# Bands of the first layer's attention: a quarter read back in one whole transfer instead of four partial ones

## The reference

```
logits  = bond_logits - 10.0 * damage            # [b, head, t, 64], of gelu(strain @ W ...)
logits  = where(t - 63 + j >= 0, logits, -inf)
weights = softmax(logits, axis=-1)               # over the window, j = 0..63
out     = einsum('bntd,bntde->bnte', weights, val_win)   # val_win[t, j] = val[t - 63 + j]
x = x + out @ W_cproj + ffn(xn)                  # ffn: 16 experts, top 4
```

## Time and profile before

| what | us |
|---|---|
| median of 3 runs (1136.08 to 1141.26) | 1139.98 |
| the profiled execution, its own time | 1139.31 |
| its span | 1137.6 |
| PE busy in the span | 974.3 |
| DVE busy | 909.8 |
| ACT busy | 787.7 |
| POOL busy | 561.9 |
| band stage of group 0 | 301.4 to 376.6 |
| band stage of group 1 | 626.0 to 707.3 |

### The profile page before, as it was taken

One profiled execution on the slowest core, in us unless ns is written; L12 is line 12 of the kernel. 1 busy time (PEld: TensorE's weight loads), 2 busy tenths in 40 slices (PEclk: granted clock), 3 DMA queues, 4 the chain that ended last, 5 costly groups with the idle time before them and its releaser, 6 DMA issues. The chain is left out here.

```text
span 1137.6 us, 23649 instructions
## 1 busy us (share of the span) xinstructions
PE 974.3 (86%) x9302; PEld 519.0 (46%) x9302; DVE 909.8 (80%) x1006; ACT 787.7 (69%) x859; POOL 561.9 (49%) x571
## 2 busy tenths in 40 slices
PE   5787778889778799999987688998999999989897
PEld 3522222233467344333333578634645465555533
DVE  7888888899777999999996867677686667476857
ACT  3689999999764899999997532432366656555574
POOL 6088888528637558888886523407720000000172
PEclk9889999999989999999999688997799999999999
DMA  8891011012188212222210784000314344432121
GB/s 292 229 376 37 31 36 33 22 39 67 39 226 193 77 58 72 71 73 73 74 55 34 203 218 118 4 1 22 98 49 130 94 120 139 122 102 84 38 59 45
DMA packets 102597, 109.56 MB, mean 96 GB/s; under 512 B 11893, under 2 KB 87121, under 8 KB 98769
## 3 DMA queue, kind: packets, MB, share of 16 engines
q1 hardware_dynamic: 93492, 87.67, 26.8%
q0 software_dynamic: 7424, 20.20, 5.9%
q10 hardware_dynamic: 1571, 0.20, 0.1%
HBM read 62.29 MB, written 42.59 MB: 92 GB/s over the span
## 5 line engine op out<-in xcount | busy, mean ns | idle before, releaser
L262 DVE SCALAR_TENSOR_TENSOR ring<-AD,PT 128x1808 f32<-128x1808 f32 (+15 forms) x128 | 282.2, 2221 | 28.1 <-PE LG L985 27.3
L985 PE MATMUL LG<-ring,lred 128*32 128x456 f32 (+15 forms) x2048 | 237.2, 583 | 0.0
L268 POOL DMA_INDIRECT ys<-rows,goali x80 | 162.1, 2027 | 72.3 <-DVE rows L869 49.4
L2362 DVE TENSOR_REDUCE MX<-SS 128x2 f32<-128x1024 f32 x119 | 144.5, 1218 | 55.6 <-PE SS L2079 55.5
L2292 ACT ACTIVATE EX<-SS 128x1024 f32<-128x1024 f32 x128 | 130.3, 1031 | 79.3 <-PE SS L2079 78.8
L925 ACT ACTIVATE ring<-ring 128x3680 f32<-128x3680 f32 (+15 forms) x47 | 161.2, 3429 | 3.6 <-DVE ring L262 3.6
L1010 PE MATMUL SD<-DSf,eyes 99*32 99x456 bf16 (+15 forms) x1280 | 96.3, 377 | 66.4 <-ACT ring L930 63.1
L931 ACT ACTIVATE ring<-ring 128x1824 f32<-128x1824 f32 (+15 forms) x80 | 145.8, 1822 | 0.0
L1996 POOL DMA_INDIRECT XN<-ys,sloti x16 | 16.4, 1024 | 246.8 <-PE SS L2089 242.2
L778 POOL DMA_INDIRECT xs<-rows,sloti x64 | 121.7, 1902 | 30.5 <-issue 19.2
L985 PEld LDWEIGHTS LG<-ring,lred 128*32 128x32 f32 x2048 | 61.5, 111 | 99.1 <-issue 76.2
(11 more groups left out here) (434 smaller groups left out, 1720.6 us busy)
## 6 DMA issues: line engine op xcount, KB each, us to landing
w1s<-in_L_ffn_W SPq DMA_DIRECT2D x39, 256.0 KB, 3.0
w2s<-in_L_ffn_W SPq DMA_DIRECT2D x39, 256.0 KB, 3.0
band<-Z SPq DMA_DIRECT2D x8, 1024.0 KB
xl<-xs SPq DMA_DIRECT2D x20, 272.0 KB, 3.1
xs<-Z SPq DMA_DIRECT2D x5, 1024.0 KB, 9.7
w1s<-w1d SPq DMA_DIRECT2D x80, 64.0 KB
w2s<-w2d SPq DMA_DIRECT2D x80, 64.0 KB
ring<-band SPq DMA_DIRECT2D x12, 384.0 KB, 9.5
```

The lines of the kernel that those rows point to most:

```text
L262: return v.scalar_tensor_tensor(out=tile[:, s, :, t0:T], in0=AD[:, s, :, j + t0:j + T], scalar=extra, in1=AD[:, s, :, PAD + t0:PAD + T], o ...
L268: pool.indirect_dma_start(ys0[:, :], bass.IndirectOffsetOnAxis(ap=goali[:, 4 * n + a:4 * n + a + 1], axis=0), yo[:, n % 2, a, :], None, bo ...
L985: mm = pe.matmul(LG[32 * b:32 * b + 32, par, s, t0:T], lred[:, s, n % 4, :], ring[:, slot, s, b, t0:T], start=(n % 4 == 0), stop=(n % 4 == 3))
L2362: v.tensor_reduce(MX[:, t, p // 2, hh:hh + 2], pairs_of(b, name), AX.X, ALU.max).then_inc(freed[slot], 1)
```

## The change

`read(k)` becomes one DMA, issued by SP: all 128 rows of `band[k]`, 128 slots each, 2 MB, over 128 partitions of 16 KB. POOL issues no band reads any more. Since every slot of `wide` is now written, the clearing of the three buffers and its semaphore go. The semaphores `d_band_in` are one per quarter instead of two. POOL's other work closes up: in group 0 both stores come first, in group 1 all eight `gate_rows` stand in a row.

```diff
-            def landed(k, half):
-                return d_in[k][half], 16 * (64 // BLK) * (g + 1)
+            def landed(k):
+                return d_in[k], 16 * (g + 1)
...
-            def read(engine, k, half):
+            def read(sp, k):
-                engine.wait_ge(wide_zero, WIDE * g + min(k, WIDE - 1) + 1)
                 if k >= WIDE:
-                    engine.wait_ge(band_pe, 8 * (M0 + k - WIDE + 1))
-                engine.wait_ge(*written(k))
-                for s0 in range(0, 64, BLK):
-                    r0 = 64 * half + s0
-                    rows = dram_rows(band, (k * P + r0) * 32 * P + 32 * s0, [[32 * P, BLK], [1, 32 * SPAN]])
-                    engine.dma_start(wide[k % WIDE][r0:r0 + BLK, s0:s0 + SPAN, :].rearrange("r s n -> r (s n)"), rows
-                                     ).then_inc(landed(k, half)[0], 16)
+                    sp.wait_ge(band_pe, 8 * (M0 + k - WIDE + 1))
+                sp.wait_ge(*written(k))
+                sp.dma_start(wide[k % WIDE].rearrange("r s n -> r (s n)"), band[k]).then_inc(landed(k)[0], 16)
...
-                clear(0)
                 if g == 0:
                     store(pool, MOE[0][7][0])
-                clear(1)
-                if g == G - 1:
-                    gate_rows(pool, 0, 0)
-                    gate_rows(pool, 0, 1)
-                read(pool, 0, 1)
-                clear(2)
-                read(pool, 1, 1)
-                if g == 0:
                     store(pool, MOE[0][7][1])
                 else:
-                    gate_rows(pool, 1, 0)
-                    gate_rows(pool, 1, 1)
-                for k in range(2, NT):
-                    read(pool, k, 1)
-                if g == G - 1:
-                    for k in range(2, K0):
+                    for k in range(K0):
                         for half in range(2):
                             gate_rows(pool, k, half)
...
-                read(sp, 0, 0)
+                read(sp, 0)
                 write(1)
-                read(sp, 1, 0)
-                for half in range(2):
-                    sp.wait_ge(*landed(0, half))
+                read(sp, 1)
+                sp.wait_ge(*landed(0))
                 write(2)
                 write(3)
                 for k in range(2, NT):
-                    read(sp, k, 0)
+                    read(sp, k)
```

More of the change, by code:

```diff
@@ L49 @@
 WIDE = 3
-BLK = 32
-SPAN = BLK + WIN
 PE_ITEMS = (1, 2, 4, 5, 7)
@@ L637, in first_layer @@
     d_out = [sem(f"d_skew{k}") for k in range(NT)]
-    d_in = [[sem(f"d_band_in{k}_{half}") for half in range(2)] for k in range(NT)]
+    d_in = [sem(f"d_band_in{k}") for k in range(NT)]
     band_pe, band_act, band_dve, vw_pe, vw_sb, nd_pe, rc_ready, att_ready = (
         sem(n) for n in ("band_pe", "band_act", "band_dve", "vw_pe", "vw_sb", "nd_pe", "rc_ready", "att_ready"))
-    wide_zero, vp_zero, side_pe, side_sb = sem("wide_zero"), sem("vp_zero"), sem("side_pe"), sem("side_sb")
+    vp_zero, side_pe, side_sb = sem("vp_zero"), sem("side_pe"), sem("side_sb")
     rct_sb = sem("rct_sb")
@@ L1429, in turn @@
                         if i == 0:
-                            for half in range(2):
-                                pe.wait_ge(*landed(k, half))
+                            pe.wait_ge(*landed(k))
                         before = max(4 * m + i // 2 - 1, 0)
```

2 lines of the change are left out of this document (removed).

## The result

The changed kernel takes **1129.88 us** (median of 5 runs, 1128.16 to 1132.02), the kernel before 1139.98 (5 runs, 1136.08 to 1141.26): a ratio of 0.991, 95% interval 0.989 to 0.993, 10.1 us less. Forecast were 1131.3 and 8.7 us. The profiled execution of the changed kernel took 1132.02 us, its span 1130.3 (1139.3 and 1137.6 before).

The account below looks back on a forecast made before the run. Read(2)'s landing, behind one queue of band transfers, was taken to bound each stage. With r (moving a 2.10 MB read) at 5.5 us, gains 19.5 - 3r and 22.2 - 3r sum to 8.7 us: 1131.3 us, range 1126.5 to 1139.5.

Parts of the forecast that it names:

- The rate: Both band stages: a whole 2.10 MB read over 128 partitions moves in 5.5 us, at 381 GB/s.
- Fixed time ahead of a read: Issue and landing cost about 1.9 us beyond movement, paid before read(0) and read(1), where the queue is empty.
- w: Time in which a band write of 1.05 MB moves, taken as 4.75 us with its ramp.
- Group 0, 3.05 us: Group 0's band stage: read(2) lands at 351.4 instead of 354.45, and all behind turn(2) moves up by 3.05 us.
- the last leg: From read(2)'s issue to turn(2): write(3), then read(2) move; the forecast's sum puts it at 10.25 us.
- it adds nothing: Write(3)'s wait for exponential 3 costs nothing: turn(0) some 3 us earlier makes it ready while write(2) still moves.
- Group 1, 5.7 us: Group 1's band stage: turn(2) 3.7 us earlier, plus 2.0 us at DVE's additions, moves turn(3) and the end up 5.7 us.
- The second step: Group 1: fetch 2 lands earlier, so DVE's two additions lose their wait and overlap: 2.4 us, of which 2.0 counted.
- The store at nothing: Group 0's second store, moved from mid-stage to its start, costs nothing or gains a few tenths.
- The rate is less than hoped: Rival: reads move at only 324 GB/s, 1137.3 us (chance 0.10), or 350 GB/s, 1134.3 us (chance 0.10).
- More bytes at the same rate, slower: Rival: reads stay at 236 to 254 GB/s while moving more bytes, 8 to 12 us lost, 1148 to 1152; chance 0.09.
- The gain is not kept: Rival: late exponential 3, or PE between turn(0) and turn(2), leaves only 2 to 4 us, 1136 to 1138; chance 0.09.

Follow-up runs that it names:

- pieces_of_32: Changed kernel with each whole read cut into four transfers of 32 partitions in the same queue: 1153.70 us, ratio 1.0118 to the kernel before.
- clears_kept: Changed kernel with the six buffer clears put back on GpSimd at the start of each stage, reads waiting for them: 1129.45 us, ratio 0.9911 to before.
- group0_only: Kernel before with the change made in group 0's band stage alone, group 1 as before: 1137.50 us, ratio 0.9974.
- after_again: The changed kernel run again unchanged as a control: 1130.50 us, ratio 0.9906 to the kernel before.
- group1_only: Kernel before with the change made in group 1's band stage alone, group 0 as before: 1131.47 us, ratio 0.9938.
- swap_g0: Changed kernel with read(2) issued ahead of write(3) in group 0: 1129.10 us, ratio 0.9894 to the kernel before.
- swap_cast: swap_g0 with ACT's second cast of the parts moved behind its copies of turn(2) in group 0: 1130.51 us, ratio 0.9913 to before.

## Why the prediction was right, and where it was only lucky

**The rate.** Right, and the base of everything: 400 to 410 GB/s in the windows against the assumed 381 and the "370 or more" named as the sign; pieces_of_32 shows that it goes when the same read is cut into transfers of 32 partitions, and clears_kept that the clears have no part in the gain. Its two bounds, 254 from partial transfers and 423 from the zeros, held it, and it lay near the upper one.

**Fixed time ahead of a read, and w.** The 1.9 us were too little for the read, and w = 4.75, taken from a write that moved at 236 GB/s, too much for a write queued behind one. turn(0) starts 8.3 to 9.5 us after read(0)'s issue, not 7.4, in the eight traces with whole reads in group 0 and the writes unchanged. But read(0) and write(1) together take 11.1 us in the changed kernel (315.15 to 326.27) where 1.9 + r + w = 12.15 were put. The read's slow start (187 GB/s in the first 2.8 us) is in no term of the sum, and write(1), at 399 GB/s, is done 2.4 us after turn(0) has begun. The two errors nearly cancel, which is luck. The sign given for turn(0), 7.0 to 7.9 us, was missed.

**Group 0, 3.05 us.** Right by group0_only (3.0, interval 0.8 to 5.1), wrong by the first trace (turn(2) at 352.11 where 351.4 was forecast, from a stage that began 2.2 us early). The failed term is the last leg: w + r = 10.25 us, for which 13.8 were taken in that execution; the median of the 15 is 11.1. Two causes are seen. The forecast had turn(0) some 3 us earlier and so exponential 3 done while write(2) still moves; turn(0) came 1.2 us earlier and at the slow clock, exponential 3 ends at 336.44, write(3) is issued then, and the DMA engines run empty meanwhile (windows of the changed kernel, columns as above):

```profile
335.00:336.00 1.00, 0.88 (x7) 0.88 (x8) 0.42 (x1) 1.00 (x1) 0.00 (x0) 1.00 1.01 418
336.00:337.00 1.00, 1.00 (x11) 1.00 (x10) 0.68 (x1) 1.00 (x3) 0.00 (x0) 1.00 0.28 107
337.00:338.00 1.00, 0.52 (x5) 0.33 (x3) 0.71 (x2) 0.36 (x1) 0.00 (x0) 1.00 0.61 139
```

In group0_only, with turn(0) at the fast clock, exponential 3 ends at 335.20 and the queue does not run dry:

```profile
335.00:336.00 1.00, 0.44 (x4) 0.45 (x5) 0.00 (x0) 0.20 (x1) 0.00 (x0) 1.00 0.97 401
336.00:337.00 1.00, 1.00 (x11) 1.00 (x10) 0.24 (x1) 0.59 (x1) 0.00 (x0) 1.00 1.09 369
```

There turn(2) is at 48.2, and the step "it adds nothing" holds. The rest of the first trace's leg, some 2.7 us against after_again, is the late end of read(2) with 1.5 MB of read(3) ahead of it; why it was so late stays open. Group 1 has the same gap as the first trace (exponential 3, then a window behind its end):

```profile
660.14 3.82 ACT L1302 ACTIVATE Z<-Z 128x2048 f32<-128x2048 f32 x1
...
664.00:665.00 1.00, 0.89 (x8) 0.70 (x7) 0.97 (x3) 0.59 (x1) 0.00 (x0) 1.00 0.42 156
```

**Group 1, 5.7 us.** Right in size and mechanism: turn(2) 3.7 us earlier forecast, 4.1 in the trace (55.5 to 51.4), 3.9 by the median of the eight traces. The second step, additions behind fetch 2, was put at 2.0 of 2.4 us: DVE's addition pair shrank from 4.18 to 2.49 and the wait of 0.66 went, 2.35 in all. The stage is 6.2 us shorter in the first pair; group1_only says 7.1, with an interval that holds 5.7.

**The store at nothing.** Wrong by 0.5 us on write(0), in the direction of a loss, covered by the scatter.

**The rivals.** "The rate is less than hoped" falls with the windows. With it falls the estimate that the prediction worked out from the DRAM figure of the Trainium skill ("DMA: Bandwidth & Descriptors", Specifications: some 358 GB/s per core): 400 to 410 were read here. "More bytes at the same rate, slower" was a good rival: the same bytes in pieces gave 1153.7, where 1148 to 1152 was written. "The gain is not kept" is half true of what comes next: swap_g0 and swap_cast show that with turn(2) another microsecond earlier ACT, then read(3), are late in its place. At r = 5.2, which 400 to 410 GB/s give, the forecast's own 41.7 - 6r is 10.5 us.

So the sum, 8.7 us, stands against 10.1 and 10.7 measured, and the difference is within what the runs tell. The mechanism is right in both groups; that the sum is so near owes something to the two errors that cancel.

## What to carry to other kernels

Give a large read all 128 partitions in one instruction, even at the price of a third more bytes and slots that nobody needs: here 2.10 MB in one piece took less time than 1.57 MB in 32-row pieces on two queues. Cutting the same bytes into pieces cost 24 us, halves on two queues 30 us, of which the moved gate multiplications are a part. Keep the partitions as the outermost dimension on both sides; an outer dimension of two put a transfer on two engines. And do not read a gain of 3 us from one pair of traces: positions in a stage moved by up to 5 us between executions, and a kernel with the change in one place alone, timed over a dozen runs, settled what the pair had wrong. Before two traces are compared, look at the granted clock in each stretch ahead of the one that matters: here 0.68 or 1.00 in turn(0) moved turn(2) by some 2 us through the exponential and the write behind it.

## What the hardware showed that was not expected

One read over 128 partitions moved at 400 to 410 GB/s, one over 64 of them at 233 with the engines as full. Halves issued on two queues within 0.3 us moved one behind the other; GpSimd's half, issued at 316.62, moved from 322 on. Writes of two transfers of 64 partitions moved at 216 alone and at 399 to 418 behind another transfer. A read's first 2.8 us showed 187 GB/s. The write with an outer dimension of two took 22.2 us for 1.05 MB. And DMAs of one queue overlap at their ends: in one execution 1.5 MB of read(3) moved before the last of read(2), issued ahead of it, had landed, in another 0.6 MB.
